# A graph attention layer on one core: two tests of adjacency tiles on GpSimd, f2 of two blocks on TensorE, and another order of the last four tiles

## What is computed

```python
in_fts = W @ inlayer.T
f1 = (w1 @ in_fts).T + b1
f2 = (w2 @ in_fts).T + b2
logits = f1 + f2.T
bias_mat = jnp.where(adj_mat > 0, 0.0, NEG_INF).astype(logits.dtype)
coefs = jax.nn.softmax(jax.nn.leaky_relu(logits) + bias_mat, axis=-1)
vals = coefs @ inlayer
x = _layernorm(x + vals, axis=-1)
```

## Time and profile before

| | us |
|---|---|
| median of three runs | 279.02 |
| the profiled execution: its time | 279.0 |
| its span, from the first instruction to the last | 277.3 |
| TensorE busy | 257.2 (93%) |
| VectorE busy | 245.8 (89%) |
| ScalarE busy | 195.6 (71%) |
| GpSimd busy | 72.2 (26%) |
| mean granted clock of TensorE | 0.983 |

### The profile page before, as it was taken

One profiled execution on the slowest core, in us unless ns is written; L12 is line 12 of the kernel. 1 busy time (PEld: TensorE's weight loads), 2 busy tenths in 40 slices (PEclk: granted clock), 3 DMA queues, 4 the chain that ended last, 5 costly groups with the idle time before them and its releaser, 6 DMA issues.

```text
span 277.3 us, 5927 instructions
## 1 busy us (share of the span) xinstructions
PE 257.2 (93%) x2163; PEld 224.5 (81%) x2163; DVE 245.8 (89%) x321; ACT 195.6 (71%) x284; POOL 72.2 (26%) x91
## 2 busy tenths in 40 slices
PE   3979949899999999999999999999999999999960
PEld 3979738688888888888888888888888888888850
DVE  1898999987998899999999999999999999999752
ACT  2669899949999999995699559955995592131310
POOL 4000046930000023002800280028002810181610
PEclk9999989999999999999999999999999999999995
DMA  6999999999999999999999999999999999101120
GB/s 198 265 303 307 307 304 291 270 270 314 319 327 327 328 326 320 319 320 322 324 344 336 345 287 275 321 310 292 337 325 326 290 271 304 45 4 34 30 68 20
DMA packets 22626, 73.64 MB, mean 266 GB/s; under 512 B 3154, under 2 KB 4308, under 8 KB 22612
## 3 DMA queue, kind: packets, MB, share of 16 engines
q1 hardware_dynamic: 11344, 35.20, 42.5%
q10 hardware_dynamic: 9860, 34.61, 41.3%
q0 software_dynamic: 1408, 3.67, 4.9%
HBM read 71.37 MB, written 2.10 MB: 265 GB/s over the span
## 4 chain that ended last, share of the span: by engine, by line
PE 39%; DVE 38%; ACT 8%; issue 8%; DMA 2%; POOL 1%; ACTq 1%; DVEq 1%; POOLq 0%
PE ps L1006 39%; DVE mn L677 11%; DVE msk L690 7%; DVE mn L682 7%; ACT sgn L448 3%; ACT bt L500 2%; DVE post L800 2%; ACT post L478 2%; DMA msk<-in_x 2%; DVE ybt L815 1%; DVE f2raw L627 1%; DVE bns L820 1%; DVE sgn L623 1%; DVE post L802 1%; DVE ntot L805 1%
## 5 line engine op out<-in xcount | busy, mean ns | idle before, releaser
L1006 PE MATMUL ps<-bt,msk 128*128 128x258 f16 x2048 | 233.0, 275 | 2.4 <-DVE msk L690 2.3
L1006 PEld LDWEIGHTS ps<-bt,msk 128*128 128x128 fp8e5 x2048 | 201.3, 98 | 33.3 <-issue 2.7
L448 ACT ACTIVATE sgn<-f2b,nf1l 128x1024 int8<-128x1024 f32 x128 | 136.6, 1147 | 5.6 <-POOL flag L391 4.3
L677 DVE TENSOR_SCALAR mn<-nat 128x4096 int8<-128x4096 int32 x32 | 73.0, 2282 | 2.2 <-DMA nat<-in_adj 1.9
L398 POOL TENSOR_SCALAR nmr<-mv 128x4 f32<-128x4 f32 x7 | 12.6, 1802 | 148.5 <-DVE mv L824 148.5
L570 ACT ACTIVATE post<-ps,ac 128x258 f32<-128x258 f32 x64 | 26.6, 470 | 25.8 <-PE ps L1006 25.8
L682 DVE SCALAR_TENSOR_TENSOR mn<-sgn,mn 128x1024 uint32<-128x1024 uint32 x32 | 39.2, 1225 | 3.8 <-ACT sgn L448 2.8
L690 DVE STREAM_TRANSPOSE msk<-mn 128x1024 uint32<-128x1024 uint32 x32 | 39.8, 1245 | 2.6
L577 ACT ACTIVATE ybt<-ybt,nmr,rstd 128x128 f32<-128x128 f32 x28 | 11.6, 485 | 30.1 <-POOL nmr L403 30.0
L695 DVE TENSOR_SCALAR msk<-msk 128x1024 uint32<-128x1024 uint32 x32 | 22.2, 695 | 1.0
L409 POOL DMA_DIRECT2D out<-ybt x24 | 21.7, 911 | 4.0 <-issue 3.8
(11 more groups left out here) (108 smaller groups left out, 110.9 us busy)
## 6 DMA issues: line engine op xcount, KB each, us to landing
nat<-in_adj SPq DMA_DIRECT2D x64, 512.0 KB, 14.0
nat<-in_adj ACTq DMA_DIRECT2D x64, 512.0 KB, 16.4
xn<-in_x POOLq DMA_DIRECT2D x4, 512.0 KB, 19.3
out<-ybt POOLq DMA_DIRECT2D x24, 64.0 KB, 7.2
msk<-in_x SPq DMA_DIRECT2D x8, 128.0 KB, 4.1
msk<-in_x ACTq DMA_DIRECT2D x8, 128.0 KB, 4.4
out<-ybt SPq DMA_DIRECT2D x4, 64.0 KB, 1.8
out<-post SPq DMA_DIRECT2D x16, 16.0 KB, 1.5
```

What stands on the lines that cost most here:

```text
L448: ins = act.activation(sgn[:, c, g * JA:(g + 1) * JA], f2b[:, :], ACT.Sign, bias=nf1l[:, bass.ds(G * t + g, 1)], scale=-1.0)
L677: dve.tensor_scalar(mn[:, c % 2], nat[:, c], 0, EDGE, ALU.is_gt, ALU.mult).then_inc(cast_done, 1)
L1006: ins = pe.matmul(ps[:, 2 * c + m, 0:2 * DV], mask_f[c][m][:, n // KB, n % KB, :], btv[m][:, n, :], start=(n == 0), stop=(n == NK - 1))
```

## The change

Six things are changed.

1. *Two tests go to GpSimd.* The entries of row tiles 1 and 2 are tested by GpSimd, with the same operation that VectorE used. Tile 1's test stands ahead of the four transfers of `xn`, tile 2's behind them and ahead of the row factors. The second waits also until VectorE has transposed tile 0, whose buffer it takes.
2. *VectorE scales chunk 1 of the plus table* instead of ScalarE (`scale_x(0, 1)` in place of `scale_act(1)`), and `split_x` waits for it.
3. *f2.* TensorE makes f2 of blocks 0 and 2, where it made blocks 0 and 1. VectorE does the other 24 columns in four pieces, the first from chunk 0 of x. The constants b1 and b2 come over ScalarE's queue, ahead of its part of x, and are spread by TensorE before `vsb` is copied.
4. *Order.* TensorE turns x block 5 before it widens the first statistics, and does block 2's columns before it turns block 3. ScalarE squares chunk 3 before the signs of tile 1. The maximum of the second statistics is taken earlier by one operation.
5. *The last quad.* Tiles 28 and 29 are done as a pair by operations of twice the width. For tiles 30 and 31 ScalarE copies only the minus sums, when they are made (a new semaphore `minus_made`), the lift is added to them, and one VectorE operation (`join`) reads the plus sums from PSUM, scales and adds. ScalarE normalises tiles 28 to 30, VectorE tile 31. The pair is stored by four transfers, tile 30 by four, and tile 31 by two from SyncE's queue and two from ScalarE's.
6. *GpSimd's loop* stores a quad before the statistics of the next, not behind them.

The core of the diff:

```diff
-                for c in range(QT):
-                    sp.wait_ge(last_ready, c + 1)
+                for i, (c, w) in enumerate(((0, 2), (2, 1))):
+                    sp.wait_ge(last_ready, i + 1)
                     for g in range(G):
-                        sp.dma_start(out_g[NQ - 1, g][:, c],
-                                     post[g * SQ:(g + 1) * SQ, 1, 0, c, 0:D]).then_inc(last_stored, 16)
+                        store_last(sp, c, w, g)
+                sp.wait_ge(tile_ready, 1)
+                for g in range(G // 2):
+                    store_last(sp, QT - 1, 1, g)
...
-            pool.dma_start(brow[:, 0:1], b1.partition_broadcast(1)).then_inc(brow_in, 16)
-            pool.dma_start(brow[:, 1:2], b2.partition_broadcast(1)).then_inc(brow_in, 16)
...
+            def cast(t, c):
+                pool.wait_ge(cast_done, t)
+                pool.wait_ge(nat_in[c], 16 * A)
+                if t >= 2:
+                    pool.wait_ge(turn_done, t - 1)
+                pool.tensor_scalar(mn[:, c % 2], nat[:, c], 0, EDGE, ALU.is_gt, ALU.mult).then_inc(cast_done, 1)
+
+            cast(1, 1)
 
             pool.wait_ge(f1_made, 2)
-            pool.wait_ge(cast_done, 2)
             for g in range(G):
                 pool.dma_start(xn[g * SQ:(g + 1) * SQ, :, :], x_g[g]).then_inc(xn_in, 16)
+            cast(2, 2)
 
...
                 with pool.Fori(1, NQ // 2) as turn:
+                    store(2 * turn - 2, 0)
                     rows(2 * turn - 1, 1)
-                    store(2 * turn - 2, 0)
+                    store(2 * turn - 1, 1)
                     rows(2 * turn, 0)
...
+                for i, (c, w) in enumerate(((0, 2), (2, 1), (3, 1))):
+                    pool.wait_ge(last_var_ready, i + 1)
+                    pool.tensor_tensor(rstd_l[:, c:c + w], vpe_l[:, c:c + w], mhalf[:, 0:w],
                                        ALU.pow).then_inc(last_rstd_ready, 1)
+                    if c < QT - 1:
+                        pool.tensor_scalar(nmr_l[:, c:c + w], mv[:, 1, c:c + w, 0], -1.0, None,
+                                           ALU.mult).then_inc(last_scale_step, 1)
+                        pool.wait_ge(last_scale_step, 2 * i + 1)
+                        pool.wait_ge(last_rstd_ready, i + 1)
+                        pool.tensor_tensor(nmr_l[:, c:c + w], nmr_l[:, c:c + w], rstd_l[:, c:c + w],
+                                           ALU.mult).then_inc(last_scale_step, 1)
...
+            act.dma_start(brow[:, 0:1], b1.partition_broadcast(1)).then_inc(brow_in, 16)
+            act.dma_start(brow[:, 1:2], b2.partition_broadcast(1)).then_inc(brow_in, 16)
...
+            square(3)
             split_x(1, 2)
             signs(1, 1, between=lambda: split_x(1, 3))
-            square(3)
             rows_out()
             scale_act(0)
             split_x(0, 0)
             act.wait_ge(cast_done, 2)
             load_far(QT + 1, 1)
-            scale_act(1)
...
-                for c in range(QT):
-                    evacuate(NQ - 1, 1, c)
-                    if c == 2:
-                        normalise(NQ - 2, 0)
+                def evacuate_minus(c):
+
+                    t = NT - QT + c
+                    act.wait_ge(minus_made, t - EARLY + 1)
+                    act.activation(post[:, 1, 1, c, :], ps[:, 2 * c + 1, 0:2 * DV], ACT.Copy,
+                                   scale=ac[:, 1, t:t + 1]).then_inc(sums_out, 1)
+
...
+                evacuate(NQ - 1, 1, 0)
+                evacuate(NQ - 1, 1, 1)
+                evacuate_minus(2)
+                normalise(NQ - 2, 0)
+                normalise_last(0, 0, 2)
+                evacuate_minus(3)
+                normalise_last(1, 2, 1)
+                act.wait_ge(tile_ready, 1)
+                for g in range(G // 2, G):
+                    store_last(act, QT - 1, 1, g)
...
-            xv_product(1)
-            f2_sum(1)
-            dve.wait_ge(b12_made, 1)
-            dve.tensor_copy(b12[:, :], ps[:, 6, D + 2:D + 4]).then_inc(b12_ready, 1)
-            xv_product(2)
-            f2_sum(2)
-            dve.wait_ge(b12_ready, 1)
+            f2_products(0, KB, 2 * KB)
+            f2_products(1, 3 * KB, 4 * KB)
+            f2_products(2, 2 * CN, 3 * CN)
...
+            f2_products(3, 3 * CN, 4 * CN)
+            dve.wait_ge(f2_made, 1)
+            f2_biased(ps[:, 7, F2_AT[1]:F2_AT[1] + KB], 2 * KB, 3 * KB)
...
-            cast(1, 1, 0)
             combine(1, 1)
...
             low_den(0)
+            scale_x(0, 1)
+            stat_max(1, 2, 4)
             scale_x(0, 2)
-            stat_max(1, 2, 4)
             scale_x(0, 3)
...
-            cast(2, 2, 0)
             combine(2, 2)
-            dve.wait_ge(y_act, 2)
+            dve.wait_ge(y_act, 1)
+            dve.wait_ge(y_ready[0], 3)
             turn(2, 2)
             plus(2, 2)
             cast(3, 3, 0)
             combine(3, 3)
-            dve.wait_ge(y_ready[0], 2)
...
+                def lift(c):
+
+                    dve.wait_ge(sums_out, QT * q + c + 1)
+                    low = post[:, s, 1, c, DV:2 * DV]
+                    step(dve.tensor_tensor(low, low, xeps[:, :], ALU.add))
...
+                    dve.wait_ge(sums_made, t + 1)
+                    dve.wait_ge(last_step, steps)
+                    step(dve.scalar_tensor_tensor(out=post[:, s, 0, c], in0=ps[:, 2 * c, 0:2 * DV],
+                                                  scalar=ac[:, 0, t:t + 1], in1=post[:, s, 1, c], op0=ALU.mult,
+                                                  op1=ALU.add))
...
+                dve.wait_ge(sums_out, QT * q + 2)
+                step(dve.tensor_tensor(post[:, s, 0, 0:2], post[:, s, 0, 0:2], post[:, s, 1, 0:2], ALU.add))
...
+                finish(0, 2)
+                lift(2)
+                join(2)
+                finish(2, 1)
+                lift(3)
+                join(3)
+                finish(3, 1)
+                dve.wait_ge(last_rstd_ready, 3)
+                rows = post[:, s, 0, QT - 1, 0:D]
+                dve.tensor_scalar(rows, rows, mv[:, s, QT - 1, 0:1], rstd_l[:, QT - 1:QT], ALU.subtract,
+                                  ALU.mult).then_inc(tile_ready, 1)
...
+                    if b in F2_PE:
+                        to, v = ps[:, bank, n - n0:n - n0 + apart_by + 1:apart_by], vsb[:, D:D + 2]
...
+            pe.wait_ge(brow_in, 32)
+            pe.matmul(ps[:, 6, D + 2:D + 4], ones[0:1, :], brow[:, :], start=True, stop=True).then_inc(v_made, 1)
...
+            f1_columns(2)
             turn_x(3)
-            f1_columns(2)
...
+            turn_x(5)
             widen_stats(0, 0, 2)
-            turn_x(5)
...
-                    edge_sums(c, 1)
+                    edge_sums(c, 1).then_inc(minus_made, 1)
```

158 lines of the change are left out of this document (84 added, 74 removed).

## The result

The changed kernel takes 296.81 us (median of four runs, 296.24 to 298.38); the kernel before took 279.02 in the same comparison (278.89 to 279.62). The ratio is 1.064, with a 95% interval of 1.059 to 1.069: slower, where 273.5 was forecast and 280.5 was the end of the range. The profiled execution took 298.4, with a span of 296.7.

What follows compares the result with a forecast made beforehand. TensorE's unbroken 214.96 us run of 30 tiles was taken as fixed, so only start and tail could move: 279.0 - 2.5 (start) - 3.0 (tail) = 273.5 us, range 271.8 to 280.5.

Steps and rivals of the forecast that it cites:

- The frame: Whole time as TensorE's start of tile 2 (53.26), 30 tiles (214.96) and tail (9.1); only first and last can move.
- I take the affine select ...: 6.6 us, ends 3.4 and 13.1: Start: length of one 4096-element test on GpSimd, 6.6 us by the affine select's slope, bounds 3.4 and 13.1.
- I take the row: a fifth, 1.3 each: Start: each GpSimd test holds VectorE for a fifth of its span, 1.3 us; 0.8 lost after waits.
- Rival 1: Start: VectorE is stopped for the whole of each GpSimd test, giving 284.1 us; chance 0.20.
- Rival 2: Start: GpSimd's test far slower, without a hold; 275.1 at 9 us, 282.5 at 13.1; chance 0.07.
- f2 ... at nothing (-0.3 to +0.3): Start: f2 of blocks 0 and 2, and b's transfers on ScalarE's queue, change nothing, -0.3 to +0.3 us.
- The signs 0.9 earlier by x block 5: Start: ScalarE's signs for tile 1 come about 0.9 us earlier, as TensorE turns x block 5 before widening the statistics.
- One scaling more on VectorE: Between transposes of tiles 1 and 2: VectorE gains one chunk to scale, 1.15 us, and no longer waits 0.42 for ScalarE.
- The tail, 3.0: After TensorE's last matmul: earlier total and two stores on each of two queues save 3.0 us, 6.1 instead of 9.1.
- Its cover: Tail: VectorE begins the last four tiles at 257.68 and is free at 263.8, before TensorE's new end at 265.7.
- The 12.4 us between the two transposes: Start: VectorE's transposes of tiles 1 and 2 lie 12.4 us apart instead of 14.25.

Runs made afterwards that it cites:

- The probe: Not the layer, x copied to the output: GpSimd tests alone, whole or in pieces, and beside single VectorE operations; 4096 entries alone took 13.99 us.
- the kernel with pieces: The changed kernel with each of GpSimd's two tests cut into eight pieces of 512 entries: 297.73 us, ratio 1.066.

## Why the prediction was wrong

- *The frame was right.* Start, 30 tiles, tail: the run of 214.96 stayed, and the loss is in the start.
- *"I take the affine select ...: 6.6 us, ends 3.4 and 13.1"*: failed. The test takes 14.1, above even the upper end. The slope of 3.2 ns between two small TENSOR_SCALAR operations, put aside as scatter, was that of the very operation moved, and came within 8% of the measured 3.4. Going by the likest operation would have given 13.1.
- *"I take the row: a fifth, 1.3 each"*: failed, and this is the larger error. VectorE was held for 24.1 us, not 2.6. The 0.04 us came from GpSimd's operation of four elements; what is held so shortly cannot be read as a share of a long one. The probe shows a product beside a test of 1024 entries held for 0.2 and beside one of 4096 for 10.6: not proportional. GpSimd's 3.26 showed the lock from its other side.
- *Rival 1* was the mechanism. Its formula, twice the test less 5.1, gives 23.1 at 14.1 us, against 20.4 measured for the start; that each hold ended 1.5 us before its test would make up for it. (Its own dates, 61.4 against 53.1, are 8.3 apart, not 8.1, so the formula should read less 4.9.) The price was missing, not the idea: at the 13.1 of the forecast's own upper bound it would have said 297. It deserved more than 0.20. The rule of the Trainium skill that spoke against the change ("SBUF — State Buffer", section "Who interferes with whom") held here for operations with two SBUF inputs and for the masking, all but the last 1.5 us of the first kind. The Trainium skill's "GPSIMD Engine Reference", section 4.1, with one-input work at roughly line rate, did not: 14.1 us, not 3.4.
- *Rival 2* (far slower, no hold) was half right: the test was far slower. Without the hold its length accounts for about 10 of the 20.4 (the estimate above); at 13.1 the rival itself had 282.5. That the kernel with pieces, which hold little, lost as much is due to the stretching of the pieces to 16.3 and 19.4.
- *"f2 ... at nothing (-0.3 to +0.3)"*: failed in size. The place of b1 and b2 alone cost 1.6 us. The prediction let the two transfers cost ScalarE's queue "up to 1 us" and took that as covered by the landing of tiles 1 and 2. But the head waits for x: in the run with b on ScalarE's queue x came 1.65 later and tile 2 began 1.54 later.
- *The signs 0.9 earlier by x block 5*: right. Against the last quad alone, the signs of tile 1 ended 1.0 earlier (34.20 instead of 35.20) and tile 2 began 1.0 earlier. *One scaling more on VectorE* and the rest of the order gave nothing (275.98 beside 275.21).
- *The tail, 3.0*: right by itself (2.8), but 1.05 in the changed kernel. Its cover was gone: VectorE ended the moments ahead of the last quad at 283.35, 5.3 before TensorE, where it was 10.5 before. So it came to the last join 1.3 late. The prediction's date of 257.68 was too early in any case: with the last quad alone VectorE began on it at 260.89, 7.6 before TensorE's end, and that still covered it. In the changed kernel:

```profile
283.35 0.66 DVE L938 TENSOR_TENSOR post<-post 128x516 f32<-128x516 f32 x1
...
289.58 0.29 DVE L922 TENSOR_TENSOR post<-post,xeps 128x129 f32<-128x129 f32 x1 [0.36 <-ACT post L632]
289.98 0.49 DVE L929 SCALAR_TENSOR_TENSOR post<-ps,ac,post 128x258 f32<-128x258 f32 x1
```

- *The 12.4 us between the two transposes*: right, 71.72 - 59.33 = 12.39.

Left open: the combine of tile 1 is shown from 45.12, 1.6 before GpSimd's second test starts, and would have ended before it by its usual 1.2; yet it was held to 1.5 before that test's end. With the tests alone moved, the same combine was not held.

## What to carry over

Price an operation that changes engine by the same kind of operation on the new engine, even if the only rows are small, and never by a milder relative. Before giving GpSimd long work, list which VectorE operations run beside it: those with two SBUF inputs wait for nearly all of it, and one of 0.26 us can cost ten. In a head where all engines meet, look also at who stands last in each queue: two transfers of 4 bytes ahead of x cost 1.6 us, and a flag that GpSimd made 4.6 us later left TensorE waiting for 2.4.

## What the runs showed that was not expected

- A VectorE product that a GpSimd test holds ends 1.5 us before the test does, for 1024, 2048 and 4096 entries. An operation of 32 elements was held to 2.4 before the end (47.88 against 50.31). With an operation's own time taken off, both come to one figure: what is held gets to run 2.7 us before the end of the test (56.16 against 58.91, 47.62 against 50.31). That would be why pieces of 512 (1.92 us) hardly hold it; no run tests this. VectorE in turn stretched such pieces from 15.15 for eight to 16.3 and 19.4 in the kernel, and four of them to 8.4 and 12.7.
- A masking with one SBUF input and two constants was held for the whole test (13.83 instead of 0.69), a transpose or a reduction of the same size not at all.
- On GpSimd an operation with two steps costs 3.4 ns an element, the same for the three kinds of number tried. From int32 to int8, one step costs 2.6 and a copy 0.9.
